# A scan kernel on one core: at the passage from batch 0 to batch 1, four pieces of work change their place in the engines' programs

## The reference, cut to what matters

```python
u  = silu(conv4(ctx @ in_proj.T) + conv_b)            # (4, 256, 256)
dt_low, B, C = split(x_proj @ u)                      # 8, 16 and 16 rows
dt = softplus(dt_proj @ dt_low + dt_b)                # "delta"
for l in range(256):                                  # the scan, 16 states per channel
    state = state * exp(dt[l] * A) + dt[l] * u[l] * B[l]
    y[l]  = sum over the states of state * C[l]
x1 = x + (y + D * u) * silu(layernorm(x))             # the gate
h  = layernorm(gelu(silu(bitlinear(layernorm(x1), w1, b1)))) * g + b
out = x1 + bitlinear(h, w2, b2)
```

## Time and profile before

| | |
|---|---|
| three runs of the kernel | median 204.08 us (202.42 to 204.76) |
| the profiled execution | 201.8 us, of which the span from first to last instruction is 200.0 us |
| VectorE busy in the span | 166.7 us (83%) |
| ScalarE busy | 166.5 us (83%) |
| TensorE busy | 157.7 us (79%), granted clock 0.927 of full speed on the mean |
| GpSimd busy | 140.3 us (70%) |

### The profile page before, as it was taken

How to read it: one execution, slowest core, us unless ns; L and a number is a source line. 1 busy time by engine, 2 the same in 40 slices (tenths; PEclk the granted TensorE clock), 3 DMA queues, 4 the chain that set the end, 5 groups by cost and what they waited for, 6 DMA issues and landing times.

```text
span 200.0 us, 3377 instructions
## 1 busy us (share of the span) xinstructions
PE 157.7 (79%) x1162; PEld 118.0 (59%) x1167; DVE 166.7 (83%) x249; ACT 166.5 (83%) x267; POOL 140.3 (70%) x135
## 2 busy tenths in 40 slices
PE   7788989969859998997876896968659927936682
PEld 5566668848647784675755584647455715404671
DVE  0587999994999889999999979997979588887650
ACT  0676999999998999999999979499495937899752
POOL 4000089999363977929999999999969888855740
PEclk9987999999988999999999999999979995996588
DMA  5808995439615000441532441200000000000011
GB/s 165 309 7 334 400 418 241 8 82 390 166 2 210 0 3 0 158 160 66 49 125 88 134 147 47 96 0 26 3 0 0 0 0 26 3 30 0 26 54 52
DMA packets 20193, 20.13 MB, mean 101 GB/s; under 512 B 13448, under 2 KB 16976, under 8 KB 19536
## 3 DMA queue, kind: packets, MB, share of 16 engines
q1 hardware_dynamic: 19584, 19.15, 29.4%
q10 hardware_dynamic: 592, 0.77, 1.3%
HBM read 17.70 MB, written 2.21 MB: 100 GB/s over the span
## 4 chain that ended last, share of the span: by engine, by line
PE 28%; ACT 24%; POOL 23%; DVE 12%; issue 10%; DMA 1%; POOLq 0%; ACTq 0%; DVEq 0%
POOL st L822 11%; ACT dA L670 7%; DVE st L976 6%; PE ps L503 5%; PE ps L443 5%; PE ps L580 4%; POOL w_raw L858 3%; PE ps L598 2%; PE ps L591 2%; PE ps L542 2%; ACT w_raw L686 2%; ACT w_raw L703 2%; PE ps L584 2%; PE ps L453 2%; DMA inw_sb<-inwT 1%
## 5 line engine op out<-in xcount | busy, mean ns | idle before, releaser
L822 POOL TENSOR_TENSOR st<-st,bc 128x1024 f32<-128x1024 f32 x32 | 76.3, 2400 | 16.8 <-DVE st L976 16.5
L976 DVE TENSOR_TENSOR_SCAN st<-dA,ps 128x1024 f32<-128x1024 f32 x32 | 71.8, 2270 | 2.3 <-PE ps L503 2.2
L503 PE MATMUL ps<-diagB,dtuT 64*128 64x128 f32 x512 | 42.9, 298 | 13.3 <-DVE st L976 11.6
L670 ACT ACTIVATE dA<-dt,negA 128x255 f32<-128x255 f32 x128 | 52.8, 494 | 0.1
L503 PEld LDWEIGHTS ps<-diagB,dtuT 64*128 64x128 f32 x512 | 33.6, 193 | 24.0 <-DVE st L976 15.0
L542 PE MATMUL ps<-id_f,st 128*128 128x128 f32 x256 | 33.3, 276 | 3.6 <-POOL st L822 3.3
L542 PEld LDWEIGHTS ps<-id_f,st 128*128 128x128 f32 x256 | 28.1, 140 | 6.7 <-POOL st L822 5.2
L591 PE MATMUL ps<-id_f,w_raw 128*128 128x128 f32 x64 | 11.3, 335 | 11.2 <-ACT w_raw L730 7.3
L591 PEld LDWEIGHTS ps<-id_f,w_raw 128*128 128x128 f32 x64 | 9.4, 175 | 13.0 <-issue 8.3
L580 PE MATMUL ps<-rows_sb,diag 128*128 128x512 f32 x32 | 16.7, 646 | 0.4 <-ACT w_raw L703 0.4
L443 PE MATMUL ps<-ctx_sb,taps_sb 128*128 128x256 f32 (+3 forms) x48 | 14.3, 463 | 0.0
(11 more groups left out here) (122 smaller groups left out, 284.0 us busy)
## 6 DMA issues: line engine op xcount, KB each, us to landing
bc<-spread SPq DMA_DIRECT2D x16, 512.0 KB, 4.5
diagB<-dblocks SPq DMA_DIRECT2D x3, 1024.0 KB, 4.7
rows_sb<-rows SPq DMA_DIRECT2D x1, 1664.0 KB, 15.6
x_nat<-x SPq DMA_DIRECT2D x2, 512.0 KB, 7.1
w_raw<-w1T SPq DMA_DIRECT2D x1, 1024.0 KB, 9.1
w_raw<-w2T SPq DMA_DIRECT2D x1, 1024.0 KB, 11.0
dblocks<-diagB SPq DMA_DIRECT2D x1, 1024.0 KB, 14.4
out<-res SPq DMA_DIRECT2D x8, 128.0 KB, 1.7
```

What stands on the lines that cost most here:

```text
L503: mm = nc.tensor.matmul(o[:, i:i + SG // 2, t, r, :], dtuT[rows, b % 2, h, t, :], diagB[rows, b % 2, t, n, :], start=True, stop=True)
L670: e = nc.scalar.activation(dA[:, k % DA_RING, i * L + 1:(i + 1) * L], dt[:, h, b % 2, 1:L], ACT.Exp, scale=negA[:, h, n:n + 1])
L822: tt(s, s, bc[:, ng].rearrange("p s l -> p (s l)"), ALU.mult).then_inc(prod_done, 1)
L976: nc.vector.tensor_tensor_scan(st[:, k % ST_RING, :], dA[:, k % DA_RING, :], slot(k), 0.0, ALU.mult, ALU.add).then_inc(scanned, 1)
```

## The change

Only the tables change. `dt_neg:2`, `clip_weights:0`, `gate:0`, `gate:1`, `dt_mask:2` go from VectorE's entry 8 to entry 9, behind scan 8. `x1:0` goes from entry 8 to entry 10, beside `x1:1`. GpSimd's `dt_series:2` goes behind prod 8. On TensorE the products of unit 8 go from entry 8 to entry 7, ahead of `sum_states` of unit 7, and `turn_z:0` goes behind that sum. ScalarE's and SyncE's programs are the same.

```diff
@@ VECTOR_AT
     "",
-    "dt_neg:2 clip_weights:0 gate:0 gate:1 dt_mask:2 x1:0",
-    "",
-    "x1:1",
+    "",
+    "dt_neg:2 clip_weights:0 gate:0 gate:1 dt_mask:2",
+    "x1:0 x1:1",
     "dt_sum:2 ln1:0",
@@ PE_AT
-    "turn_z:0",
-    "scale_b:8 scale_rest:8 scale_b:9 scale_rest:9 scale_b:10 scale_rest:10 convolve:3 scale_b:11 "
+    "scale_b:8 scale_rest:8",
+    "turn_z:0 scale_b:9 scale_rest:9 scale_b:10 scale_rest:10 convolve:3 scale_b:11 "
     "scale_b:12 xdbl:3 scale_rest:11 scale_rest:12 turn_du:2",
```

## The result

| | before | after |
|---|---|---|
| median of the comparison | 203.25 us (201.9 to 204.76, 4 runs) | 206.98 us (204.94 to 208.98, 4 runs) |
| ratio | | 1.0196, 95% 1.0145 to 1.0247 |
| profiled execution, its span | 201.8, 200.0 us | 204.94, 203.1 us |
| TensorE's granted clock, mean | 0.927 | 0.929 |

The changed kernel is slower by 1.96% in this comparison. With the forecast of 206.7 us (204.7 to 208.8) the time agrees, but not all of that is merit. The forecast was 2.6 us on top of a median of 204.08 us. Here the kernel before has 203.25 us, so the medians lie 3.73 us apart. The lower base hides most of that difference. The sum behind the forecast agrees less well than the time, as will be seen.

A forecast was written before the change was run, and what follows sets the result against it. No engine full: a chain of waits through `convolve:3` on TensorE, with ScalarE fullest in the passage. 1.27 + 2.3 − 1.8 + 0.9 + 1.0 − 1.1 = 2.6 us, 1.3%, on the 204.08 median makes 206.7 us (204.7 to 208.8).

The forecast's parts named there:

- Step 1: VectorE ahead of scan 8: idle about 4 us, ended by TensorE's L503, scan 8 at 51.6; 1.24 us lost.
- Step 2: ScalarE: unit 9's exps start at 55.8, +2.0 us, with no wait for `convolve:3`; `silu_u:3` and `xdbl:3` 1.3 us late.
- Step 3: Port shared by VectorE and GpSimd: clipping and prod 8 meet behind scan 8, scan 9 at about 60.1, +2.3 us.
- port costs more: Rival at the shared port: prod 8 goes ahead of L983 and TensorE's clock falls, +3.9 to +4.7 us; chance 0.15.
- Step 4: What arrives behind the clipping group: `add_b2:0` 3.6 us late, scan 13 about 3 us late.
- VectorE's old waits, up to `dt_neg:3`: VectorE behind scan 10: earlier waits for TensorE and ScalarE (0.61, 0.16, 0.84 us) take up delay, -1.8 us.
- `dt_neg:3` meets prod 11: Shared port: `dt_neg:3`, ready at 73.9, meets prod 11, which runs until about 74.9, and loses 0.9 us.
- `root1:0` late for `quant1:0`: GpSimd's three small steps come behind prod 11, between the second clipping, and end up to 1 us after it: +1.0 us.
- the mask of 81.4 loses less: VectorE's later mask, which lost 1.48 us to a prod before, loses less to prods 12 and 13: -1.1 us.
- the port costs little: Rival: only the later start counts, +1.3 us, or 205.4 us; chance 0.17.
- the chain over `convolve:3` decides: Rival, not slower: earlier scan 8 brings `convolve:3` forward, at most 0.69 us gained, 203.4 us; chance 0.06.
- Later meetings at the port: Rival, not slower: later prod and mask meetings fall otherwise, loss shrinks to 0.3 us, 204.4 us; chance 0.10.

The follow-up runs named there:

- e3: Changed kernel with GpSimd's part undone, `dt_series:2` again ahead of prod 8: passage (scan 7 to scan 16) 45.71 us, median 205.81 us, ratio 1.0039.
- e11: e3 with dummy products on TensorE in its waits ahead of unit 11, unit 12 and `xdbl:3`: passage 44.84 us, median 203.59 us, ratio 0.9933.
- e10: The changed kernel run once more, nothing altered: passage 47.36 us, median 207.19 us, ratio 1.0015.
- e13: Kernel before with 20 dummy products on TensorE ahead of unit 10's products: passage 42.93 us, median 202.85 us, ratio 0.9975.
- e2: Kernel before with VectorE's and GpSimd's parts of the change, without TensorE's: passage 48.68 us, median 206.59 us, ratio 1.0259.
- e4: Changed kernel with 30 and 12 dummy products on TensorE ahead of units 11 and 12: passage 49.07 us, median 206.76 us, ratio 1.0184.
- e6: Changed kernel with `xdbl:3` ahead of `scale_b:12` on TensorE: passage 47.40 us, whole time 208.05 us (one run).
- e12: The kernel before profiled a second time, nothing altered: passage 46.55 us, whole time 204.4 us (one run).
- e14: The kernel before profiled a third time, nothing altered: passage 44.70 us, whole time 206.82 us (one run).
- e1: Kernel before with TensorE's part of the change alone: passage 44.21 us, median 205.54 us, ratio 1.0192.
- e8: Changed kernel with `clip_weights:0` moved ahead of scan 8, into VectorE's gap: passage 47.29 us, whole time 208.85 us (one run).
- e9: Kernel before with ScalarE reordered to free it earlier, and VectorE's gates and x1 one entry later: passage 43.98 us, whole time 205.64 us (one run).

## Why the prediction was right, and where not

**Step 1, the idle time, was right.** Predicted: VectorE idle for 4.03 us and scan 8 at 51.6. Measured: 4.00, ended by L503, and 51.18 + 0.39 = 51.57. The loss against the 2.79 us of before is 1.21 (predicted 1.24 to 1.27).

**Step 2, ScalarE's start, was right, its further course not.** The exps of unit 9 start at 55.28 + 0.39 = 55.67 (predicted 55.8), and there is no wait for `convolve:3`. But I then let ScalarE be 1.2 to 1.3 us late for the rest. In fact `xdbl:3` stands behind `scale_b:12`, which waits for scan 10. After the waits of 3.69 and 1.61 us both ran at 0.50. ScalarE got `xdbl:3` 3.0 us late (68.52 + 0.39 against 65.91). I had named these waits and a possible fall, "at nothing, at worst 0.8 us", but looked only at the sum of unit 8 behind them. Measured between e3 and e11 the fall costs 0.87 us. The way that I had named, over the sum of unit 8 to scan 12, is the one that it took in e10 (0.96 us of waiting), not in the first profile. The cost of 0.87 us is of the sort that the kernel before has at `convolve:3`, where e13 measures 0.75. So TensorE's clock brought nothing on balance, as predicted, but for another reason: by e13 there is a gain to be had at `convolve:3`, and it was paid back at `xdbl:3`. The fall was moved, not removed.

**Step 3, the port, was right in kind and 0.55 us too small.** VectorE's group grew by 2.16 (L983), 0.29 (L985) and 0.40 us (mask), together 2.85 where I took 2.3 and had 3.6 as the upper bound. Scan 9 is at 60.24 + 0.39 = 60.63 (predicted 60.1). The order was not the one that I took from the row of 72.54. L983 followed L920 without a gap, and yet prod 8 had gone ahead of it. I had also read that row as "whichever comes second waits", but in it L833, the one that waited, had started 0.20 us ahead of L983. This is the order of the "port costs more" rival, at a price between the two, because L813 and L815 cost only 0.29 and 0.40 us beside L985 and the mask. The Trainium skill's "SBUF — State Buffer" (Who interferes with whom) lets the order of issue decide. Prod 8 was started at 53.61 and L983 at 53.96, so this place agrees with it, and e3 agrees that the lock is what costs: with prod 8 at 57.18 the same L983 takes 1.22 us. GpSimd's 128x2 steps don't agree with it as they are recorded. In e13 L837 (the L831 of the other kernels) started 0.46 us ahead of the second clipping, which kept its 1.22 us, and in the changed kernel L831 started 1.04 us ahead of L985 and was done at 77.87, 0.04 us after it. What lets a prod go first and not these steps isn't shown. The lower bound of the prediction was also added up too low: 56.9 + 2.36 + 0.41 is 59.7, so +1.9 and not +1.6. The sum doesn't use it.

**Step 4, what arrives behind, came out near by errors of both signs, which is luck.** The terms, in us:

| term | predicted | measured |
|---|---|---|
| idle ahead of scan 8 | +1.27 | +1.21 |
| the port behind scan 8 | +2.3 | +2.88 (scan 10 at +4.09) |
| VectorE's old waits, up to `dt_neg:3` | -1.8 | -1.09 (`dt_neg:3` at +3.00) |
| `dt_neg:3` meets prod 11 | +0.9 | 0 |
| `root1:0` late for `quant1:0` | +1.0 | +0.22 (scan 13 at +3.22) |
| the mask of 81.4 loses less | -1.1 | -0.15 |
| sum | +2.6 | +3.07 |

The waits that I had named add up to 1.61 us (0.61 + 0.16 + 0.84), so that even 1.8 was more than the rows gave. In the run they gave back less, since L920's wait for ScalarE (0.84 before) is still 0.81: ScalarE had become late with it. For the same reason `dt_neg:3` came at 74.74, when prod 11 was just over (70.13 + 4.68 = 74.81), and L920 has its 0.69 us. `root1:0` did run beside the clipping, as said (L831 2.30 us instead of 0.73), but VectorE waited only 0.31 us for it. And the mask took 1.74 us instead of 1.89: the two prods beside it were as late as the mask itself. `add_b2:0`, predicted 3.6 us late, is 68.91 + 0.39 against 65.31, that is 3.99 late, by the 0.4 to 0.5 us that the port cost more.

**The rivals.** That the port costs little is out (2.85 us). That the chain over `convolve:3` decides is out: scan 8 started at 51.57, 1.2 us behind the 50.36 at which it would have had to start. Later meetings at the port did not disappear. The dear case was half right: its order and its fall of the clock both happened, and the sum stayed below it.

**An account of the 3.07 us in experiments.** With the clock kept in both kernels and no prod 8 in the way, e13 to e11 is 42.93 to 44.84, +1.91. VectorE's rows say the same: 1.21 of idle time and 0.70 that L985 and the mask lose to L813 and L815 (they have 1.52 and 0.83 us there too). The fall behind scans 9 and 10 adds 0.87 (e11 to e3). Prod 8's meeting adds 1.04 (e3 to after). The fall that the kernel before had and the changed one has not takes off 0.75 (e13 to before). 1.91 + 0.87 + 1.04 - 0.75 = 3.07. That the four close is no test, since each step begins where the last one ends. Each step is one pair of profiles. By e10 the passage after varies by 0.6 us with the length of the fall, and the kernel before by more, so the terms of about 1 us are known to no better than that. What is firm is the meeting itself: L983 took 3.38 or 3.39 us in all five profiles with prod 8 in its way (after, e2, e4, e6, e10) and 1.22 in e3 and e11.

**The measure itself.** The 3.07 us are against the shortest of three profiles of the kernel before, and 46.55 of e12 is only 0.20 us shorter than 46.75. The profiles alone would give a difference of 0.2 to 3.7 us, by which way mask and L815 fall and how long the clock stays low. Their means, 44.98 us of three before and 47.06 of two after, lie 2.1 us apart. The whole times bear out the sign in the first comparison and in the medians of all runs (207.2 against 203.9 us), but the two intervals, 1.0145 to 1.0247 and 0.9924 to 1.0106, exclude each other, so the size stays open. How often the mask wins in unprofiled runs isn't known. In four profiles of kernels with before's order here (the first, e12, e13, e14) it won twice.

**Versions.** e11 is better than the changed kernel by 1.91 us and e13 by 3.82 us of passage. Against the kernel before neither is faster by more than its interval.

## What to carry to other kernels

An operation moved out of an idle gap doesn't only take its own time with it: ask what the other engine at the shared port does in the gap and what it does at the new place, and in which order both become ready. Where moved work makes TensorE wait, look past the wait for the small step that stands behind it in TensorE's program and that another engine wants (here `xdbl:3`). A stall removed at one place and its low clock may just turn up at a later one, as here at scans 9 and 10. And where whole times scatter by more than the effect, measure the distance between two instructions that frame the change, in more than one profile of either kernel, and compare the granted clock of the same stretches before you explain what is left.

## What the runs showed of the hardware that I had not expected

- Two engines that want the shared port within 0.02 us of each other get it in either order, with the same program: L925 took 0.42 us beside an L815 of 1.56, or 1.52 us beside one of 1.26. GpSimd's was recorded 0.02 us earlier in both. At scan 11 the kernel is then 1.0 us late in e14 and 2.9 in e12. Of the 1.9 us between these two 0.30 come from a longer L920, and the rest goes with the clock, which was low for longer in e12.
- An operation that follows its predecessor on VectorE without a gap (L983 behind L920) still let a prod that had been started 0.35 us earlier go first, and took 2.16 us longer for it.
- With the granted clock at 0.50 for most of their time the 16 products of `convolve:3` took 5.2 and 5.8 us instead of 3.70 (before, e12), and the 4 of `xdbl:3`, at 0.50 throughout, 1.93 instead of 1.03 to 1.06. In e11 and e13 dummy products in the waits for the scans kept the clock at 1.00 from 56 to 78 us. In e4 they kept it to 72 us and it fell behind the next wait.
- The start and the end of the kernel vary for all kernels alike: scan 7 starts between 44.24 and 46.97 us, and from scan 31 to the end there are 47.3 to 49.3 us in some profiles and 50.4 to 50.8 in others, with both in the kernel before (48.3, 48.6, 50.8) and in the changed one (49.0, 50.8). This is as large as the whole effect.
- The granted clock goes with both. Scan 7 starts at 44.2 to 44.9 us in the three profiles whose clock was 1.00 from 0 to 44 us (after, e3, e12), at 45.0 to 45.9 in the six with 0.96, and at 46.1 to 47.0 in the five with 0.92. The end is 47.3 us in the two with 1.00 from 147 to 158 us (e2, e3), 47.6 to 49.3 in the six with 0.84, and 50.4 to 50.8 in the six with 0.69 (e1, e6, e8, e9, e10, e14). What makes the clock differ there between profiles of one program isn't shown.
